# The third division of probabilities goes ahead of the addition of the main MLP's result in VectorE's order

## What is computed

```python
def attn(x):                                   # per row: 512 x 256
    h = layernorm(x) * g1 + b1
    q, k, v = split(h @ qkv_w + qkv_b)         # 16 heads of 16
    s = window_scores(q, k) / 4                # a window of 15 keys
    p = softmax(s)                             # exp(s - max) / sum
    x = x + (window_sum(p, v) @ proj_w + proj_b)
    m = layernorm(x) * g2 + b2
    return x + (gelu(m @ fc1_w + fc1_b) @ fc2_w + fc2_b)

def moe(x):
    main = gelu(x @ W1m + b1m) @ W2m + b2m
    gate, two = top2(softmax(mean(x) @ w_gate + b_gate))
    e = sum(gate[k] * (gelu(x @ W1e[two[k]] + b1e) @ W2e[two[k]] + b2e) for k in (0, 1))
    return a * main + (1 - a) * e              # a = clip(alpha)

x = x + attn(layernorm(x))
x = x + moe(layernorm(x))
```

## Time and profile before

| | |
|---|---|
| median of 3 runs | 2013.59 us (2012.11 to 2015.28) |
| the profiled execution's own time | 2011.87 us |
| its span, first to last instruction | 2010.1 us |
| PE busy | 1980.8 us, 99% |
| PE weight loads busy | 1813.9 us, 90% |
| DVE busy | 1475.0 us, 73% |
| ACT busy | 1135.5 us, 56% |
| POOL busy | 928.1 us, 46% |
| granted TensorE clock, mean | 0.998 |

### The profile page before, as it was taken

The page is one execution under the profiler, slowest core; times in us unless marked ns, Lnnn a source line. Parts: engine busy times, 40 slices in busy tenths (PEclk is TensorE's granted clock), DMA queues, the critical chain, the costliest instruction groups (busy, mean ns, idle before and its releaser), DMA issues.

```text
span 2010.1 us, 37531 instructions
## 1 busy us (share of the span) xinstructions
PE 1980.8 (99%) x13454; PEld 1813.9 (90%) x13454; DVE 1475.0 (73%) x2462; ACT 1135.5 (56%) x1801; POOL 928.1 (46%) x909
## 2 busy tenths in 40 slices
PE   7899999999999999999999999999999999999999
PEld 6789999999999999999999999999999999999998
DVE  8687786867868687786877868678686776868753
ACT  5465555646556565565555556455565655655554
POOL 6436155362543635245361553625436353453625
PEclk9999999999999999999999999999999999999999
DMA  3121110212102121121211102121021211212121
GB/s 111 43 64 53 52 50 27 74 54 58 53 28 73 43 74 43 45 56 37 75 53 50 51 27 74 53 58 52 29 71 45 74 44 41 60 38 74 43 59 53
DMA packets 188848, 108.79 MB, mean 54 GB/s; under 512 B 65436, under 2 KB 187640, under 8 KB 188664
## 3 DMA queue, kind: packets, MB, share of 16 engines
q1 hardware_dynamic: 187316, 105.43, 18.5%
q10 hardware_dynamic: 1348, 0.98, 0.2%
HBM read 85.52 MB, written 8.39 MB: 47 GB/s over the span
## 4 chain that ended last, share of the span: by engine, by line
PE 92%; DVE 4%; issue 2%; ACT 1%; POOL 1%; DMA 0%; ACTq 0%; POOLq 0%; DVEq 0%
PE psB L233 50%; PE psA L233 25%; PE psA L1082 5%; PE psA L1109 5%; PE psA L1094 3%; PE psA L1001 2%; DVE pr L622 1%; DVE smax L618 1%; DVE acc L560 1%; POOL wm_lo L425 0%; DVE hr_lo L544 0%; POOL wf_lo L425 0%; PE psA L1126 0%; DVE rinv L620 0%; DMA raw<-in_L_attn_qkv_w 0%
## 5 line engine op out<-in xcount | busy, mean ns | idle before, releaser
L544 DVE TENSOR_TENSOR hr_lo<-hf,hr_hi 128x512 fp32r<-128x512 f32 x512 | 494.4, 966 | 427.8 <-ACT hr_hi L851 427.3
L851 ACT ACTIVATE hr_hi<-hf 128x512 fp32r<-128x512 f32 x512 | 323.8, 632 | 273.0 <-PE psB L233 184.8
L436 POOL TENSOR_TENSOR wx_lo<-raw,wx_hi 128x512 fp32r<-128x512 f32 x256 | 396.7, 1549 | 21.4
L434 POOL TENSOR_SCALAR wx_hi<-raw 128x512 fp32r<-128x512 f32 x256 | 186.4, 728 | 357.3 <-PE psB L233 343.3
L847 ACT ACTIVATE hf<-psB,b1x 128x512 f32<-128x512 f32 x256 | 175.1, 684 | 199.4 <-PE psB L233 198.4
L233 PE MATMUL psB<-wx_hi,hr_hi 128*128 128x256 f32 x1024 | 287.5, 281 | 0.2
L233 PE MATMUL psB<-wx_hi,hr_lo 128*128 128x256 f32 x1024 | 286.3, 280 | 0.0
L233 PE MATMUL psB<-wx_lo,hr_hi 128*128 128x256 f32 x1024 | 285.7, 279 | 0.0
L450 POOL TENSOR_SCALAR kb<-kT 64x384 f32<-64x384 f32 x128 | 81.3, 635 | 357.5 <-ACT kT L867 349.6
L233 PE MATMUL psB<-z_hi,wx_hi 128*128 128x512 f32 x512 | 210.9, 412 | 0.0
L233 PE MATMUL psB<-z_hi,wx_lo 128*128 128x512 f32 x512 | 202.5, 395 | 0.0
(11 more groups left out here) (153 smaller groups left out, 5126.8 us busy)
## 6 DMA issues: line engine op xcount, KB each, us to landing
raw<-in_L_ffn_W1e SPq DMA_DIRECT2D x256, 128.0 KB, 2.2
raw<-in_L_ffn_W2e SPq DMA_DIRECT2D x256, 128.0 KB, 2.2
out_x<-acc SPq DMA_DIRECT2D x32, 256.0 KB, 2.2
xin<-in_L_attn_x SPq DMA_DIRECT2D x15, 512.0 KB, 3.8
vb<-vs SPq DMA_DIRECT2D x64, 96.0 KB
vb<-vs SPq DMA_DIRECT2D x62, 80.0 KB
tm<-in_L_ffn_b2e SPq DMA_DIRECT2D x32, 128.0 KB, 3.0
raw<-in_L_attn_fc_w SPq DMA_DIRECT2D x8, 256.0 KB, 4.1
```

The source lines that it names most:

```text
L434: g.tensor_scalar(wx[0][:, s, :], raw[:, s, :], 1.0, 0.0, ALU.mult, ALU.add).then_inc(w_hi.sem, 1)
L436: g.tensor_tensor(wx[1][:, s, :], raw[:, s, :], wx[0][:, s, :].bitcast(f32), ALU.subtract).then_inc(w_lo.sem, 1)
L544: v.tensor_tensor(hr[1][:, c % 2, :], hf[:, c % 3, :], hr[0][:, c % 2, :].bitcast(f32), ALU.subtract).then_inc(h_lo.sem, 1)
L851: a.activation(hr[0][:, c % 2, :], hf[:, c % 3, :], ACT.Copy).then_inc(h_hi.sem, 1)
```

## The change

In DVE's loop the `if` that calls `gather` moves from ahead of the steps of slots 3, 9, 12 and 15 to behind them. `gather` is called in slots 9, 17 and 33 alone, and of the steps moved past only `normalise(t, 2)` has one of these slots. So the one difference in DVE's instructions is in slot 9 of t = 1 to 15: the three instructions of `normalise(t, 2)` now come ahead of the two of `gather(t, 7)`. No instruction is added or removed, and no other engine's order changes.

```diff
@@ -738,8 +738,6 @@
             for t in range(ROWS + 1):
                 f = t - 1
                 for q in range(NQ + 2):
-                    if q >= 2 and there(ORDER[q - 2][0], t) and ORDER[q - 2][0] == "f" and ORDER[q - 2][1] % KH == KH - 1:
-                        gather(t, ORDER[q - 2][1])
                     if t < ROWS:
                         if q == 3:
                             normalise(t, 0)
@@ -747,6 +745,8 @@
                             normalise(t, 2)
                         elif q == 15:
                             norm2_apply(t, 1)
+                    if q >= 2 and there(ORDER[q - 2][0], t) and ORDER[q - 2][0] == "f" and ORDER[q - 2][1] % KH == KH - 1:
+                        gather(t, ORDER[q - 2][1])
                     if q < NQ and there(ORDER[q][0], t):
                         h_low(t, *ORDER[q], q)
                     if q == 0:
```

## The result

The kernel after takes 2023.99 us in the median of 6 runs (2022.88 to 2024.95), the kernel before in the runs beside them 2013.32 (2012.11 to 2015.28). The ratio is 1.0052, with a 95% interval from 1.0039 to 1.0065. The forecast was 2023.0, 9.45 above the median of before; measured were 10.7. The profiled execution took 2024.83 us, 12.96 more than that of before (2011.87).

What follows compares the result with a forecast made beforehand. PE was taken as the bound, busy 122.02 of 122.22 us a turn. New wait 0.89 plus restart 0.10 less freed 0.36 is 0.63; fifteen times that, 9.45, on the median 2013.59 gives 2023.0 us, range 2019.0 to 2027.2.

Steps and rivals of the forecast that it cites:

- Its mechanism at slot 9: Turn(2) stops waiting for the division, but down f8 waits for the later addition: +0.63 us per turn of the loop.
- What bounds the kernel: PE bounds the loop, busy 122.02 of 122.22 us a turn; a delay in its single file goes through to the end.
- The old wait goes: At turn(2), PE's wait for the third division (L622) vanishes because the division comes first: 0.36 us gained per turn.
- The new wait: Down f8 waits for the first half of the addition, starting at 1008.99 and not 1008.10: 0.89 us per turn.
- The restart: After waiting, down f8 takes longer because its second matmul starts late: 0.10 us per turn, at least nothing.
- What stays: Behind turn(2) PE gets nothing back, DVE's sum is unchanged and turn(3) gains room: the whole 0.63 us goes through.
- Rival A (faster): At down f8 the new wait is shorter than the old; full gain 5.4 us, 2008.2; 3 in 100.
- Rival B (the delay is taken up): PE has hidden slack of 0.6 us in a turn of the loop; time stays at 2013.6; 4 in 100.
- Rival C (the port): Moved GpSimd splits hold DVE's two-operand instructions, such as the fourth division's L622; turn(3) 1.6 us late, 2047; 7 in 100.

Runs made afterwards that it cites:

- e2: The kernel after, with GpSimd's key copies (L450) from t = 1 waiting for the second division's multiply; 2016.56 us, ratio to before 1.0026.
- e1: The kernel before, with GpSimd's key copies (L450) from t = 1 waiting for the second division's multiply; 2006.66 us, ratio to before 0.9982.
- e10: e2 with the third division's reduce and reciprocal left out (output differs); 2000.47 us, ratio to before 0.9948.
- e11: e1 run once more, unchanged, for the level of its set; 2006.79 us, ratio to before 0.9979.
- e7: e2 with the reciprocal of the third division left out (output differs); 2012.05 us, ratio to before 0.9984.
- e8: e2 with attended(1) cut in two from t = 1, its last two instructions behind the addition, and ACT's attended_high(0) later; 2001.89 us, ratio to before 0.9941.
- e4: e1 with the addition cut in two, first half ahead of the third division, second half behind it; 2015.95 us, ratio to before 1.0029.
- e5: The kernel before, unchanged, profiled a second time; 2008.82 us in one execution.
- e6: The kernel after, unchanged, profiled a second time; 2024.00 us, ratio to before 1.0045.
- e3: The kernel before, with a memset of one column of an unused tile ahead of the second division; 2013.76 us, ratio to before 1.0016.

## Why the prediction was right

Its mechanism at slot 9 held, and its size: 0.63 a turn was forecast and 0.64 measured (e2 against e1), though two terms were off and cancelled. What it had wrong is that nothing else in the loop would move. That its number still came out within 1.0 us has luck in it. Both are told below.

**What bounds the kernel.** Right. PE was the one file that everything goes through; what it lost came out at the end.

**The old wait goes.** Right: no wait of L1094 from t = 1 on. Its 0.36 is confirmed from the other side by e10, in which it is freed with no new wait: turn(2) comes 0.36 earlier than in e11 and ends 0.40 earlier. A turn gains only 0.28, since turn(3) stands hard on the fourth division there (its multiply ends at 1006.90 + 0.96 = 1007.86, turn(3) starts at 1007.91), and 0.14 of the gain goes at that place.

**The new wait.** 0.89 was forecast and 1.00 measured. Two parts of the term are as worked out: L618 starts 0.07 before attended(1)'s end (1012.25 against 1010.80 + 1.52 = 1012.32), and from there to the addition it is 2.13. The mis-sized part is PE's reaction. I took 0.05 from the turn; here the first half ends at 1014.38 + 0.74 = 1015.12 and PE starts at 1015.27, 0.15 later; e2, e7 and e8 have the same 0.15. In e4, where the second half is the one waited for, it is 1010.05 against 1009.26 + 0.74 = 1010.00, so 0.05 again. A difference in the code is that the first half has two waits ahead of it (for h_low and for the addition) and the second half one; no run separates that.

**The restart.** 0.10 forecast; the down took 0.08 more.

**What stays.** Turn(2) came 0.69 later and not 0.63, but a turn of the loop is only 0.64 longer (e2 against e1). Matmul by matmul, e2's turn(2) starts 0.70 later than e1's; 0.04 come back within turn(2), 0.05 at turn(3) and 0.04 at attend(3), and from there to the next addition 0.07 are lost again. Turn(3) had been hard on the fourth division, as the prediction said, and has room now. That PE gets nothing back is thus not quite so, and the two misses cancel.

**Rival A (faster).** It falls with e7: the wait follows the division's length one for one, down to nothing at 1.50 if that holds on, which is where the prediction put the point at which the sign turns. e10's 0.87 is beyond it and gains, and the kernel, with 2.14, is on the wrong side.

**Rival B (the delay is taken up).** It falls with e2: without the port a turn is 0.64 longer than in e1.

**Rival C (the port).** Right as a mechanism, wrong as to the place. At slots 9 to 11, where I looked for it, the moved splits do no harm; in after L641 takes 0.68 and h_low of f10 0.69, where they took 1.10 and 1.79. Where it struck, slot 3, nothing had been moved. Its rule that a held L622 ends 0.81 behind GpSimd's end comes out there: in after's turn above the third copy ends at 1112.64 + 0.50 = 1113.14 and the multiply at 1112.65 + 1.30 = 1113.95. The step that failed is the sentence that PE has no later gap and so nothing else matters: it asked where the delay could be taken up, but not which of the places that were just on time could tip over. The two waits for L587 in the earlier trace rows were the trace of one, and the sentence that PE has no wait behind turn(2) passed them by. In the profiled execution this adds 13 turns of 0.35, 4.5 us; the other terms are 15 x 0.64 = 9.6 and a start that is 0.95 earlier (up f9 of t = 1 at 147.70 against 148.65), together 13.2 against 12.96 measured.

So the median of 2023.99 lies 1.0 from the forecast because slot 9 was sized right and, by luck, because the 2013.59 that it was added to seems to hold most of what the port costs already. From a before as beside e1 (2010.60) the same 9.45 would have given 2020.05, and the median of after would lie 3.9 from that. How much the port adds in timed executions is an estimate, as told under e5 and e6; a profile of a timed execution would decide it.

## What to carry to other kernels

When two results of one engine are owed to a bound engine, put first the one that the bound engine's own order asks for first, and compare the two times at which it asks, not the wait that shows: the wait that shows belongs to the second claim only because the first is served. Before such a swap, work out whether what goes first is shorter than the slack (the time that it could be late at no cost) of what goes second; if not, look for something with slack of its own that can be cut and put behind both, as the second half of attended was here. And list the places that are just on time, within 0.1 us, all over the loop, since a swap can tip one that it doesn't touch.

## What the runs showed of the hardware

A two-operand instruction of DVE and a copy of GpSimd that start within some 10 ns of each other are served one after the other, and the loser stands until the winner is through: 0.34 us on DVE's side (1.30 - 0.96), 0.82 on GpSimd's (1.33 - 0.51). One memset more, which moved DVE by some 10 ns (e3), was enough for 14 of 14 to be lost. The Trainium skill speaks of this in "SBUF — State Buffer", section "Who interferes with whom": "Issue order, not op shape, decides who blocks." The trace agrees, by the recorded starts to within 4 ns: the shapes are the same in before and after, and the other one is held.

A down of 12 matmuls that has waited takes 1.48 us in place of 1.40 where its first half waits (after, e2, e7, e8): the second matmul starts 0.19 to 0.20 behind the first and not 0.12. Where the second half waits, in e4, that distance is 0.22 to 0.23.

A reduce of DVE isn't held by GpSimd: in before L611 starts at 1114.41, in the middle of GpSimd's L436 (1112.78 to 1114.61), and takes its usual 0.95.
